# Seams of a 16-layer kernel: four layers normalise the next layer's input themselves, three more take the last batch at their front, and pair attention issues the steps of this norm in another order

## The reference

```
def _layernorm(x, axis=-1, eps=1e-05):
    m = jnp.mean(x, axis=axis, keepdims=True)
    v = jnp.var(x, axis=axis, keepdims=True)
    return (x - m) / jnp.sqrt(v + eps)

x = x + layer_i(_layernorm(x, axis=-1), ...)      # i = 0 .. 15
```

```
q = softmax(be * q);  k = softmax(be * k)
kv = cumsum(einsum('zsD,zsd->zsDd', k, v), axis=1);  kn = cumsum(k, axis=1)
num = einsum('zsD,zsDd->zsd', q, kv);  den = sum(q * kn, axis=-1)
out = (num / den) @ Wo.T + bo
```

```
dA = exp(d_t[:, :, None] * A)
h = dA * h + (d_t * u_t)[:, :, None] * b_t[:, None, :]
y = einsum('bdn,bn->bd', h, c_t)
...
y = (y + u * D) * silu(z);  return y @ out_proj_w.T
```

## Time and profile before

| what | value |
|---|---|
| three runs, us | 2795.40, 2807.47, 2813.47 |
| median of the runs, us | 2807.47 |
| profiled execution: its own time, us | 2810.36 |
| its span from first to last instruction, us | 2808.6 |
| mean granted TensorE clock | 0.907 |
| span's start to end of layer 2 | 989.4 |
| pass n3, with its gaps | 989.4 to 1014.0 |
| pair attention (layer 8) | about 1502 to 1602 |
| state-space layer 10 | 1781.3 to 2093.3 |
| state-space layer 14 | 2445.3 to 2759.9 |

### The profile page before, as it was taken

How to read it: one execution, slowest core, us unless ns; L and a number is a source line. 1 busy time by engine, 2 the same in 40 slices (tenths; PEclk the granted TensorE clock), 3 DMA queues, 4 the chain that set the end, 5 groups by cost and what they waited for, 6 DMA issues and landing times. The chain is left out here.

```text
span 2808.6 us, 30635 instructions
## 1 busy us (share of the span) xinstructions
PE 2359.8 (84%) x9720; PEld 1010.9 (36%) x9760; DVE 1763.0 (63%) x2747; ACT 1270.4 (45%) x2497; POOL 645.0 (23%) x740
## 2 busy tenths in 40 slices
PE   8999999767389889779987699777779989877878
PEld 3333334312122244454553244222224447322323
DVE  4666665568877544543544544588884447478895
ACT  3555652168378721313422154355645422255653
POOL 1111110132111110211010100355550032155561
PEclk9999999879799989888678799888999999889899
DMA  3000000022000020000000000000000000000000
GB/s 147 1 1 1 1 1 1 11 39 42 2 1 1 1 90 0 1 1 1 1 1 0 0 1 0 0 1 0 0 0 1 1 1 2 1 0 1 0 0 15
DMA packets 9358, 25.92 MB, mean 9 GB/s; under 512 B 1072, under 2 KB 7280, under 8 KB 8176
## 3 DMA queue, kind: packets, MB, share of 16 engines
q1 hardware_dynamic: 8336, 23.18, 2.9%
q10 hardware_dynamic: 864, 0.79, 0.2%
HBM read 16.56 MB, written 1.05 MB: 6 GB/s over the span
## 5 line engine op out<-in xcount | busy, mean ns | idle before, releaser
L3222 PE MATMUL l_py<-l_read,w_const 128*128 128x512 f32 x512 | 316.0, 703 | 93.2 <-DVE l_read L3355 74.8
L3499 POOL TENSOR_TENSOR l_drive<-l_du,l_bsb 128x512 f32<-128x512 f32 x256 | 326.1, 1296 | 208.0 <-ACT l_bsb L3296 187.9
L3346 DVE TENSOR_TENSOR_SCAN l_state<-l_decay,l_drive 128x512 f32<-128x512 f32 x256 | 310.2, 1212 | 60.8 <-ACT l_decay L3304 53.2
L398 ACT ACTIVATE l_probs<-l_psp,l_stats 128x512 f32<-128x512 f32 x256 | 172.9, 682 | 150.5 <-DVE l_stats L408 150.5
L3304 ACT ACTIVATE l_decay<-l_delta,l_a 128x512 f32<-128x512 f32 x256 | 176.4, 690 | 138.6 <-DVE l_state L3346 138.3
L259 POOL TENSOR_TENSOR l_nx_small<-l_nx_small,w_const 128x4 f32<-128x4 f32 x36 | 36.7, 1019 | 776.5 <-DVE l_nx_small L253 776.5
L3222 PEld LDWEIGHTS l_py<-l_read,w_const 128*128 128x128 f32 x512 | 98.4, 213 | 247.1 <-DVE l_read L3355 208.5
L1268 DVE TENSOR_REDUCE l_tops<-l_ring 128x2 f32<-128x1024 f32 x128 | 151.5, 1220 | 45.6 <-PE l_ring L1259 45.3
L406 DVE TENSOR_REDUCE l_stats<-l_psp 128x2 f32<-128x1024 f32 x128 | 156.1, 1220 | 35.9 <-PE l_psp L360 35.1
L3355 DVE TENSOR_TENSOR l_read<-l_state,l_pc 128x512 f32<-128x512 f32 x256 | 168.0, 656 | 0.0
L714 DVE SCALAR_TENSOR_TENSOR l_product<-l_psu,w_gated,l_first 128x512 f32<-128x512 f32 x104 | 78.0, 750 | 137.5 <-ACT l_first L688 137.4
(11 more groups left out here) (543 smaller groups left out, 4444.1 us busy)
## 6 DMA issues: line engine op xcount, KB each, us to landing
l_stack<-l_parts SPq DMA_DIRECT2D x84, 64.0 KB
w_gated<-in_gated SPq DMA_DIRECT2D x1, 3297.5 KB, 10.7
w_mha<-in_mha SPq DMA_DIRECT2D x1, 2568.5 KB, 13.4
w_ssm<-in_ssm SPq DMA_DIRECT2D x2, 1171.0 KB, 15.2
w_moe<-in_moe SPq DMA_DIRECT2D x1, 2248.0 KB, 18.3
w_const<-in_const SPq DMA_DIRECT2D x1, 1325.0 KB, 7.7
x<-x_in SPq DMA_DIRECT2D x1, 1024.0 KB, 4.8
out<-x SPq DMA_DIRECT2D x1, 1024.0 KB, 3.9
```

The costliest lines, as they stand in the source:

```text
L398: act.activation(probs[:, s % 4, i, :], psp[:, s % 2, i, :], ACT.Exp, bias=stats[:, s % 4, 1, i:i + 1], scale=scale, accum_out=stats[:, s ...
L3222: pe.matmul(py[:, t, :], eye, read[:, s % 4, :], start=n == 0, stop=n == NS - 1, skip_group_check=True)\
L3346: dve.tensor_tensor_scan(state[:, s % 4, :], decay[:, s % 2, :], drive[:, s % 4, :], 0.0, ALU.mult, ALU.add).then_inc(L["state"].sem, 1)
L3499: pool.tensor_tensor(drive[:, s % 4, :], du[:, b % 2, t, :], bsb[:, n % 2, :], ALU.mult)\
```

## The change

- **Tables.** Layers 2, 10 and 14 now normalise for their successors, and layers 2, 10 and 15 take the last batch of their predecessors. With that, passes n3, n11 and n15 are gone (n0 and n14 stay), and layers 3, 11 and 15 take the last batch of layers 2, 10 and 14 at their front. Layers 1 and 9 no longer normalise their last batch.
- **Keep-choice attention** takes `late` at its front and calls the norm's steps for batches 0 to 2 at x = 130 + 8b (`centre`) to 137 + 8b (`scale`). `centre` waits for all maxima (`top2`), since its bank belongs to the ring of scores.
- **State-space layer** takes `late` at its front. In the last batch it calls the steps for batches 0 and 1 at states n = 0 to 4 and 5 to 9 on PE and at the DVE steps k = 3, 6, 8, 11 and 13, 16, 18, 21. `rstd` stands behind the drives of k = 7 and 17. The steps of batch 2 stand behind the loop, around the last `project_out` and the last sum.
- **Pair attention** calls the same steps in another order.

Lines in the listings of the changed kernel are some 4 to 72 higher than before.

The diff, cut to its core:

```diff
@@ class NextNorm @@
+        self.elsewhere = elsewhere or {}
+        if buffers:
+            self.kept, self.square_sb, self.diag_sb = buffers
+            self.small = L.sb(key + "_small", [P, 2, TT])
...
     def bank(self, b):
-        return self.banks[(b - self.first) % len(self.banks)]
+        return self.elsewhere.get(b, self.banks[(b - self.first) % len(self.banks)])
@@ keep_attention @@
+        nx = NextNorm(L, ring[:, 0, :], buffers=(rest[:, 0:1, :], rest[:, 1, :], fold[:, :, :]))
+        late = NextNorm(L, ring[:, 5, :], last=True, buffers=(outs_t[:, :].unsqueeze(1), c_sb[:, :], fold[:, :, :]))
...
             if n:
                 pe.wait_ge(L["high"].sem, L["high"].at(0, n))
                 pe.wait_ge(L["rest"].sem, L["rest"].at(0, n))
+            if b == B - 1 and last_in:
+                pe.wait_ge(L["in_xn"].sem, L["in_xn"].at(0, 1))
...
+        def normed(x, later):
+
+            b, r = divmod(x - SLOTS - 2 - later, 8)
+            return b if r == 0 and 0 <= b < inner else None
+
...
                 project(pe, 0, 0)
+                if last_in:
+                    late.centre(pe, B - 1)
                 project(pe, 0, 1)
                 weight_total(pe)
+                if last_in:
+                    late.var(pe, B - 1)
+                    late.spread(pe, B - 1)
...
                     if x % 32 == 28 and x >= 60 and x - 60 < SLOTS:
                         project_out(pe, (x - 60) // 32)
+                    if normed(x, 0) is not None:
+                        pe.wait_ge(L["top2"].sem, L["top2"].at(0, SLOTS))
+                        nx.centre(pe, normed(x, 0))
+                    if normed(x, 3) is not None:
+                        nx.var(pe, normed(x, 3))
+                    if normed(x, 6) is not None:
+                        nx.spread(pe, normed(x, 6))
...
                     if x % 32 == 29 and x >= 61 and x - 61 < SLOTS:
                         finish(dve, (x - 61) // 32)
+                    if normed(x, 2) is not None:
+                        nx.keep(dve, normed(x, 2))
...
@@ pair_attention, PE @@
-                    if is_batch(a):
-                        add_below(pe, a)
                     if normed(o):
                         nx.centre(pe, o)
                     if is_batch(a):
+                        add_below(pe, a)
                         add_above(pe, a)
@@ pair_attention, DVE @@
                         scan_keys(dve, a)
+                    if normed(o - 1):
+                        nx.diag(dve, o - 1)
+                    if is_batch(a):
                         if a == 0 and last_in:
...
                         ask_below(dve, a)
+                        ask_above(dve, a)
                     if normed(o):
                         nx.keep(dve, o)
                     if is_batch(a):
-                        ask_above(dve, a)
+                        divide(dve, a)
                     if normed(o):
                         nx.eps(dve, o)
-                    if is_batch(a):
-                        divide(dve, a)
-                    if normed(o):
-                        nx.diag(dve, o)
@@ state_space @@
+        nx = NextNorm(L, front[:, :], elsewhere={2: pb[:, :], 3: pb[:, :]})
+        late = NextNorm(L, py[:, 0, :], last=True, shared=nx)
...
+            if b + 1 == B and n < 11:
+                i, r = divmod(n, 5)
+                if r == 0 and i < 2:
+                    pe.wait_ge(L["done"].sem, L["done"].at(i, 1))
+                    nx.centre(pe, i)
+                if r == 2:
+                    nx.var(pe, i)
+                if r == 4:
+                    nx.spread(pe, i)
...
             def _(pe):
+                if last_in:
+                    late.centre(pe, B - 1)
                 pe.wait_ge(L["taps"].sem, L["taps"].at(0, 1))
                 project_x(pe, 0, 0, (0, 1, 2, 3))
+                if last_in:
+                    late.var(pe, B - 1)
                 project_x(pe, 0, 1, (0, 1, 2, 3))
+                if last_in:
+                    late.spread(pe, B - 1)
...
+                pe.wait_ge(L["bsb"].sem, L["bsb"].at(0, B * NS))
+                nx.centre(pe, B - 2)
+                nx.var(pe, B - 2)
                 project_out(pe, B - 1)
+                nx.spread(pe, B - 2)
...
+                        if not ahead and n in (1, 6):
+                            nx.square(act, n // 5)
...
+                        if b + 1 == B:
+                            i, r = divmod(k, 10)
+                            if r == 3 and i < 2:
+                                nx.keep(dve, i)
+                            if r == 6 and i < 2:
+                                nx.eps(dve, i)
+                            if r == 8 and i < 2:
+                                nx.diag(dve, i)
+                            if r == 1 and 1 <= i <= 2:
+                                nx.scale(dve, i - 1)
...
                 add_skip(dve, B - 1)
+                nx.keep(dve, B - 2)
                 gate(dve, B - 1)
+                nx.eps(dve, B - 2)
+                nx.diag(dve, B - 2)
                 finish(dve, B - 1)
+                nx.scale(dve, B - 2)
...
+                        if b + 1 == B and k in (7, 17):
+                            nx.rstd(pool, (k - 7) // 10)
+                nx.rstd(pool, B - 2)
@@ tables @@
-NORMALISES_NEXT = (0, 1, 3, 4, 5, 6, 7, 8, 9, 11, 12)
-NORMALISES_LAST = (1, 3, 4, 5, 6, 7, 8, 9, 11, 12, 13)
+NORMALISES_NEXT = (0, 1, 2, 3, 4, 5, 6, 7, 8, 9, 10, 11, 12, 14)
+NORMALISES_LAST = (1, 2, 3, 4, 5, 6, 7, 8, 9, 10, 11, 12, 13, 15)
```

More of the change, by code:

```diff
@@ L1546, in _ @@
                                 .then_inc(L["ones_rows"].sem, 1)
+                        if b == 0 and i and last_in:
+                            late.rstd(pool, B - 1)
                         if b == 0 and i:
@@ L1557, in _ @@
                     lower_parts(pool, n)
+                for b in range(inner):
+                    nx.rstd(pool, b)
             @block.sync
@@ L3405, in _ @@
                     .then_inc(L["a_exp"].sem, 1)
+                if last_in:
+                    late.square(act, B - 1)
                 for t in range(CT):
```

65 lines of the change are left out of this document (56 added, 9 removed).

## The result

| | median of the runs, us | lowest to highest | runs |
|---|---|---|---|
| before | 2806.74 | 2792.61 to 2818.07 | 20 |
| after | 2790.84 | 2785.01 to 2802.46 | 20 |

A forecast was written before the change was run, and what follows sets the result against it. No single engine: PE at its clock in passes, chains in pair attention and at seams, DVE in state-space last batches. Terms summed to -27.5, from 2810.4 to 2782.9; less 2.9 for the profiled run's offset, 2780.0 us, range 2771 to 2789.

The forecast's parts named there:

- A: Pair attention, batches 0 to 2: the new order removes DVE's waits for PE, -20.0 us, bounds -10.2 and -25.
- R4: Rival, chance 0.10: pair attention stays at half clock throughout, saving only 10.2 us, kernel at 2789.8.
- E and F: Seams 10 to 11 and 14 to 15: norm steps cost more than the passes saved, +5.0 and +5.5 us.
- The +1.5 at the end: End of pair attention: eps and pow, formerly under the reciprocal, come late, costing 1.5 us.
- B: Layer 1 to 2: the last batch's norm chain goes, hidden in layer 2's front, -9.2 us, bounds -8.5 to -10.5.
- C: Layer 9 to 10: the 8.6 us chain goes and layer 10's front gains clock, -9.7 us, bounds -8 to -10.
- The deferred batch: Fronts of layers 3, 11 and 15: taking the predecessor's last batch costs 2.6 us per routed layer, 3.0 per cell.
- D: Layer 2 to 3: the 21.7 us pass goes against costs at layer 2's end and layer 3's front, +0.9 us.
- R2: Rival, chance 0.12: layer 3's front gets its full clock early, 6.5 us less, kernel at 2773.5.
- the +13.0 for two norms: Last batch of layers 10 and 14: DVE work plus stalls, 6.1 us for the first norm, 6.9 for the second.
- R1: Rival, chance 0.12: norms in state-space layers cost their DVE work alone, 3.8 us instead of 13.0 per layer, kernel 2761.6.
- R3: Rival, chance 0.06: DVE stalls drop PE's clock to half in state-space last batches, 27 us per layer, kernel up to 2834.

The follow-up runs named there:

- pair_only: The kernel before with only the new order of pair attention, tables unchanged: 2782.8 us, ratio 0.9924.
- fronts: The kernel before with only layers 2 and 10 taking the last batch of layers 1 and 9 at their fronts: 2783.9 us, ratio 0.9930.
- no_ssm: The changed kernel with layers 10 and 14 not normalising for their successors, passes before 11 and 15 back: 2769.1 us, ratio 0.9866.
- ssm_later: The changed kernel with every norm step of the state-space layers called later in the last batch: 2760.4 us, ratio 0.9832.

## Why the prediction was right and where it was not

- **A, pair attention, -20.0.** Right in mechanism and size: 22.0 in the profile, 18.5 with pair_only alone. The period was put at 15.2 at full clock and 20.1 at half, with a third of the time at half; they were 15.5, 15.3 and 18.9. R4 (half clock throughout) is out, although the measured 2790.8 lies nearest to its 2789.8: that is chance, since E and F made up the difference. The +1.5 at the end is seen: the last diag waits for POOL.
- **B, layer 1 to 2, -9.2.** Right in mechanism, but more than its bound of -10.5: -10.3 in layer 1 and -2.0 in the front of layer 2. The chain took 8.6 as forecast; the rest of layer 1's gain stands in its first 26 us, where PEclk was 0.93 before and 1.00 after. And the first product of layer 2 behind it took 2.08 (L1031), and 1.12 (L1039) without it. The forecast had taken such a gain from the clock for layer 10 and not for layer 2.
- **C, layer 9 to 10, -9.7.** Its own terms add up to -9.6. The chain goes (8.5 in fronts, 6.8 in the table). The first product group of layer 10 (L3206, before L3152) did gain, 3.69 us instead of 5.51, but the front did not: from its start to the first scan it took 26.8 us, against 25.8 before. The forecast had looked at PE alone; DVE's diag took 4.06 us there (last section). With that C is -5.8, short of its bound of -8. B and C together came out at -18.1 for a forecast of -18.9, which is luck.
- **The deferred batch.** 3.1 us in layer 15 (33.6 against 30.5) for a forecast of 3.0. In layer 11 it is 2.6 as forecast, counted from the first norm step (169.7 against 167.1).
- **D, seam 2 to 3, +0.9.** The sum was right against a slow pass: from the third sum of layer 2 to layer 4 the changed kernel took 172.7 us, the one before 171.6. Two terms were wrong and cancelled. The end of layer 2 was put at +11.5 and measured, from the start of the third sum to that of the last, 45.1 against 27.5: +17.6. The missing 6 come with the clock, which the step "I take 2.5 for batch 0 and 9.0 for the other two" took as full. The front of layer 3 was put at +11.1 with its deferred batch, and the layer grew by 4.6, since the low spells fell mostly into layer 2 and only little into layer 3. R2, with its early clock, comes near for layer 3, but not for its reason: the spell had begun earlier and was over sooner. What the forecast took for fixed, the pass at 21.7, took 15.0 to 15.1 in three profiles.
- **E and F, seams 10 to 11 and 14 to 15, +10.5.** This is the step that failed: "That is about 4.5, and DVE is there after a read, a scan and a read, 2.5: a stall of 1.3 to 2", and with it the +13.0 for two norms. The last batch cost 19.6 us more. The keeps waited 4.6 instead of 2.6 to 4.0, the eps 6.1 instead of 4.6, and `scale`, for which the forecast had no wait at all, 2.5. DVE's work grew by 6.3 instead of 3.8: each diag took 1.20 us beside the drives of GpSimd instead of 0.69. (The terms given for one norm's work add up to 2.05, not 1.9.) Against that, the 0.75 for the power in front of a drive is not seen: DVE waits 1.3 for decays in this batch, 1.2 before. The wait before the first keep was 3.38, because the estimate let TensorE start the batch on time, while it stood 2.83 for the bank `l_py`, and its products came at a low clock. The end cost 4 instead of 2.5. Together 22 us (no_ssm). The direction was right, and R1, which had these stalls hidden, is out: 13.3 us of the 19.6 are waiting, as ssm_later shows. R3 is right in kind only: the clock fell to 0.82 with the stalls, not to 0.5.
- **The sum.** By the runs, A is about -20, B and C together -20, D 0 and the state-space seams +22: -18, against -15.9 measured and -27.5 forecast. The difference is E and F. The parts do not add up more finely than that: by the medians alone A is -25 and B and C -23.5, each with an interval of some 7 us to either side.

## What to carry to other kernels

A step that is put into another engine's queue costs its work only if it is called late enough: count from the moment at which its input can be ready, backlog of the producing engine included, and call it one or two steps later. Two norms in the same loop cost 19.6 us or 3.6, and in pair attention the order of four calls was worth 20. The steps of a pass that ran alone can cost more than the pass did, here 22 us more for two passes of 13, if they are put where they stop a full engine. Before such a change is judged as a whole, its parts should be timed apart, since here a gain of 40 us hid a loss of 22.

## What was not expected of the hardware

- **A VectorE operation beside a GpSimd one.** In the front of layer 10 diag, which takes 0.69 us elsewhere, took 4.06 while GpSimd cast 4096 columns:

```profile
1740.35 3.59 POOL L3598 CAST l_spread<-w_const 96x4096 bf16<-96x4096 f32 x1
1740.43 4.06 DVE L270 TENSOR_TENSOR l_nx_diag<-w_const,l_nx_small 128x512 f32<-128x512 f32 x1 [1.12 <-POOL l_nx_small L263]
...
1744.55 0.70 PE L278 MATMUL l_py<-l_nx_diag,w_const 128*128 128x512 f32 x1 [1.90 <-DVE l_nx_diag L270]
```

  It is issued 0.08 us into the cast and ends 0.55 us after it, and 0.69 of its own is about what is left behind the cast. PE stands 1.90 us for it, and that is about what the front of layer 10 lacks: it lost 1 us where C expected 1 us of gain. The kernel before had the like beside the same cast: the small operation on `l_a` (L3452), 0.17 us in the changed kernel, took 3.26, and nothing waited for it. The diags of the last batch took 1.20 beside the drives of GpSimd, while its scans, which take their decays from PSUM, kept their 1.21 to 1.22. The Trainium skill, page "SBUF — State Buffer", section "SBUF: two separate sides", has the rule: a VectorE operation with two inputs in SBUF and a GpSimd operation that reads SBUF exclude each other for the whole of the instruction, and the one that starts first holds the port. The cast and diag agree with it, and so do the scans, which have only one input in SBUF. It was not tried with the cast moved.
- **The clock of one stretch differs between executions of the same code.** n0 took 14.5 to 15.3 us in some of these profiles and 21.5 to 21.9 in the others. The first of the four sums of layer 2 came 306 to 316 us after the layer's start among kernels with the same code up to there. That is why single profiles differ by 23 us where the medians differ by 16, and why the parts had to be timed by medians.
- **The same products at the end of layer 2 ran at 0.75 in one order and at 1.00 in another.** Before the clock fell for the second time, at about 975, TensorE had stood 1.57 and 0.94 us for norm steps of DVE. The wait that matters for a chain is therefore longer than the latencies of its steps at full clock add up to. What exactly decides the clock was not tried.
